# Three weight buffers for the expert layers of a fused transformer, first loads during the token table, held biases, GpSimd on a quarter of the one-hots

## What is computed

```python
for e in range(E):                                  # E = 8, H = 768
    w_e = jnp.sum(top_w * (top_idx == e), axis=-1)
    h = jax.nn.silu(xf @ Wg[e].T) * (xf @ Wu[e].T)
    out = out + h @ Wd[e].T * w_e[:, None]
```

```python
h = jax.nn.gelu(jnp.einsum('bld,df->blf', x, W1e) + b1e, approximate=False)
out = jnp.einsum('blf,fd->bld', h, W2e) + b2e
y = y + ge[..., None] * out
```

## Time and profile before

| | us |
|---|---|
| median of 3 runs | 3250.55 (3246.6 to 3256.33) |
| the profiled execution | 3239.71 |
| its span, first to last instruction | 3238.0 |
| TensorE busy in the span | 2587.4 (80%) |
| VectorE busy | 1416.1 (44%) |
| ScalarE busy | 919.4 (28%) |
| GpSimd busy | 389.2 (12%) |

### The profile page before, as it was taken

How to read it: one execution, slowest core, us unless ns; L and a number is a source line. 1 busy time by engine, 2 the same in 40 slices (tenths; PEclk the granted TensorE clock), 3 DMA queues, 4 the chain that set the end, 5 groups by cost and what they waited for, 6 DMA issues and landing times. The chain is left out here.

```text
span 3238.0 us, 57118 instructions
## 1 busy us (share of the span) xinstructions
PE 2587.4 (80%) x18506; PEld 2223.7 (69%) x18506; DVE 1416.1 (44%) x3924; ACT 919.4 (28%) x2177; POOL 389.2 (12%) x486
## 2 busy tenths in 40 slices
PE   5876999955775688983999368999578989889895
PEld 5774999944664478873888256777357777777775
DVE  2346333345776511114222743555564363453634
ACT  1220222213552133321222113444123242332421
POOL 0000222210000133330000100000011010110100
PEclk8987999977995799995999558999679999999898
DMA  3002333320001355553000000000011203113021
GB/s 87 0 21 63 119 97 110 123 75 14 0 0 39 95 154 152 146 143 69 0 0 0 2 1 14 0 0 1 10 33 44 73 0 87 29 29 87 0 82 35
DMA packets 162395, 164.72 MB, mean 51 GB/s; under 512 B 24040, under 2 KB 147614, under 8 KB 162334
## 3 DMA queue, kind: packets, MB, share of 16 engines
q1 hardware_dynamic: 142334, 130.13, 14.4%
q0 software_dynamic: 11520, 27.54, 2.8%
q10 hardware_dynamic: 8480, 6.29, 0.8%
HBM read 255.23 MB, written 20.45 MB: 85 GB/s over the span
## 5 line engine op out<-in xcount | busy, mean ns | idle before, releaser
L874 PE MATMUL f_pg<-f_vxT,f_w 128*128 128x128 f32 x2112 | 265.2, 281 | 46.1 <-DMA f_b<-in_L_ffn_b 28.6
L874 PEld LDWEIGHTS f_pg<-f_vxT,f_w 128*128 128x128 f32 x2112 | 256.8, 196 | 53.8 <-issue 52.2
L887 PE MATMUL f_po<-f_wd,f_hid 128*128 128x192 f32 x1440 | 255.7, 327 | 13.1 <-DMA f_b<-in_L_ffn_b 7.9
L887 PEld LDWEIGHTS f_po<-f_wd,f_hid 128*128 128x128 f32 x1440 | 231.8, 191 | 16.5 <-ACT f_hid L925 12.3
L2225 PE MATMUL s_bank<-s_disp,s_w 96*128 96x256 f32 x768 | 174.8, 385 | 7.1 <-DVE s_disp L2321 7.1
L925 ACT ACTIVATE f_hid<-f_pg,f_b 128x128 f32<-128x128 f32 x384 | 106.2, 376 | 249.4 <-PE f_pg L880 249.4
L948 DVE TENSOR_TENSOR f_hid<-f_silu,f_pg 128x128 f32<-128x128 f32 x336 | 81.5, 284 | 214.1 <-ACT f_silu L921 199.4
L844 POOL DMA_INDIRECT f_answers<-f_vout,f_to_row x120 | 118.5, 987 | 457.9 <-DVE f_vout L960 248.1
L2236 PE MATMUL s_bank<-s_hid,s_w 128*96 128x256 f32 x768 | 171.0, 379 | 0.0
L2225 PEld LDWEIGHTS s_bank<-s_disp,s_w 96*128 96x128 f32 x768 | 147.9, 193 | 30.4 <-DVE s_disp L2321 8.8
L921 ACT ACTIVATE f_silu<-f_pg 128x128 f32<-128x128 f32 x336 | 78.1, 277 | 301.9 <-PE f_pg L880 281.5
(11 more groups left out here) (372 smaller groups left out, 4916.2 us busy)
## 6 DMA issues: line engine op xcount, KB each, us to landing
f_wd<-in_L_ffn_W SPq DMA_DIRECT2D x64, 576.0 KB
s_w<-in_w SPq DMA_DIRECT2D x128, 288.0 KB, 3.4
f_wd<-in_L_ffn_WdT SPq DMA_DIRECT2D x56, 576.0 KB
f_w<-in_L_ffn_W SPq DMA_DIRECT2D x64, 384.0 KB
f_w<-in_L_ffn_WgT SPq DMA_DIRECT2D x56, 384.0 KB
f_w<-in_L_ffn_WuT SPq DMA_DIRECT2D x56, 384.0 KB
f_wr<-in_L_ffn_W SPq DMA_DIRECT2D x128, 96.0 KB
f_wr<-in_L_ffn_WgT SPq DMA_DIRECT2D x112, 96.0 KB
```

Source lines behind the costliest of these rows:

```text
L874: pe.matmul(pg[j][:, a * ROWS:(a + 1) * ROWS], lift[a][r][:, j * 128:j * 128 + 128], xT[r][:, 0, :], start=(a == 0), stop=False, skip_grou ...
L887: last = pe.matmul(po[:, c * D:c * D + D], hid[r][:, j, c * 128:c * 128 + 128], wd[r][:, j, :], start=(at == 0), stop=(at == FC - 1))
```

## The change

- `fresh` compares with tile n - 3, and each buffer (weights, rows, transposed rows, hidden values, outputs) exists three times.
- A class `Weights` holds the weight buffers over both blocks. In `tokens_of_places` SyncE now runs `begin`, which asks for the weights of tiles 0 to 2, and in f1 all biases of all experts. In `experts` SyncE goes tile by tile: two register reads, wait until tile n - 3 was lifted, lift loads, wait until it was lowered, down load.
- The two halves of the lift weights come with one DMA for 128 partitions instead of two for 64; its DRAM side is read as (half, row, column).
- The biases of f1 aren't loaded per tile. ScalarE and VectorE read the tile's expert into a register and address the held biases with it.
- GpSimd makes at_hi for every odd pair, VectorE for the even ones; VectorE still makes all at_lo. TensorE waits for both.

The core of the diff:

```diff
-            nc.vector.tensor_tensor(passed[:, 2:NT], tile_expert[:, 2:NT], tile_expert[:, 0:NT - 2], ALU.not_equal)
-            link(nc.vector.memset(passed[:, 0:2], 1.0))
+            nc.vector.tensor_tensor(passed[:, 3:NT], tile_expert[:, 3:NT], tile_expert[:, 0:NT - 3], ALU.not_equal)
+            link(nc.vector.memset(passed[:, 0:3], 1.0))
...
+        @block.sync
+        def _(sp):
+            begin(sp)
...
+            pool.wait_ge(ready, 1)
+            for n in range(1, PAIRS_OF, 2):
+                t = n // 2
+                if n >= RINGS:
+                    pool.wait_ge(used, n - RINGS + 1)
+                nc.gpsimd.tensor_scalar(at_hi[n % RINGS][:], iota[0:H2, 0:A], hi[:, 1, t:t + 1], token[:, 1, t:t + 1],
+                                        ALU.is_equal, ALU.mult).then_inc(picked_by_pool, 1)
...
+                if n % 2:
+                    pe.wait_ge(picked_by_pool, n // 2 + 1)
...
-                nc.vector.tensor_scalar(at_hi[n % RINGS][:], iota[0:H2, 0:A], hi[:, r, t:t + 1], token[:, r, t:t + 1],
-                                        ALU.is_equal, ALU.mult).then_inc(picked, 1)
+                last = nc.vector.tensor_scalar(at_lo[n % RINGS][:], iota[0:H2, :], lo[:, r, t:t + 1], None, ALU.is_equal)
+                if r == 0:
+                    last = nc.vector.tensor_scalar(at_hi[n % RINGS][:], iota[0:H2, 0:A], hi[:, r, t:t + 1], token[:, r, t:t + 1],
+                                                   ALU.is_equal, ALU.mult)
+                last.then_inc(picked, 1)
...
-            def bring_lift(n, r, e, new):
-                sp.wait_ge(lifted, (n + 1) * PER)
-                for a, src in enumerate((w_in1, w_in2) if gated else (w_in1,)):
-                    sp.dma_start(lift[a][r][:], src[ds(e, 1), 0:128].rearrange("o p n -> p (o n)"), cond=new).then_inc(loaded[r], 16)
-                    for s in range(2):
-                        sp.dma_start(rest[a][r][64 * s:64 * s + 64],
-                                     src[ds(e, 1), 128:D, s * HALF * 128:(s + 1) * HALF * 128].rearrange("o p n -> p (o n)"),
-                                     cond=new).then_inc(loaded[r], 16)
-                if not gated:
-                    sp.wait_ge(hidden, (n + 1) * FC)
-                    sp.dma_start(bias[r][:], b1[ds(e, 1)].rearrange("o p c -> p (o c)"), cond=new).then_inc(loaded[r], 16)
-            def bring_down(n, r, e, new):
-                sp.wait_ge(lowered, n + 1)
-                sp.dma_start(wd[r][:], w_down[ds(e, 1)].rearrange("o (c p) n -> p (o c) n", p=128), cond=new).then_inc(down_loaded[r], 16)
-                if not gated:
-                    sp.wait_ge(outed, n + 1)
-                    sp.dma_start(down_bias[r][:], b2[ds(e, 1)].broadcast_to([128, D]), cond=new).then_inc(down_loaded[r], 16)
-            def of_tile(n):
-                return (sp.value_load(expert_of[0:1, ds(n, 1)], min_val=0, max_val=E - 1),
-                        sp.value_load(fresh[0:1, ds(n, 1)], min_val=0, max_val=1))
-            bring_lift(0, 0, *of_tile(0))
-            with sp.Fori(0, NT // 2 - 1) as i:
-                e = [of_tile(i * 2 + r) for r in range(3)]
-                bring_lift(i * 2 + 1, 1, *e[1])
-                bring_down(i * 2, 0, *e[0])
-                bring_lift(i * 2 + 2, 0, *e[2])
-                bring_down(i * 2 + 1, 1, *e[1])
-            bring_lift(NT - 1, 1, *of_tile(NT - 1))
-            bring_down(NT - 2, 0, *of_tile(NT - 2))
-            bring_down(NT - 1, 1, *of_tile(NT - 1))
+            def bring(n, r):
+                e, new = weights.of_tile(sp, n)
+                sp.wait_ge(lifted, (n - 1) * PER)
+                weights.bring_lift(sp, r, e, new)
+                sp.wait_ge(lowered, n - 1)
+                weights.bring_down(sp, r, e, new)
+            with sp.Fori(0, (NT - 3) // 3) as i:
+                for r in range(3):
+                    bring(i * 3 + (3 + r), r)
+            for n in range(3 + (NT - 3) // 3 * 3, NT):
+                bring(n, n % 3)
...
-                                            in_offset=bass.IndirectOffsetOnAxis(ap=from_row[:, n * RC + c:n * RC + c + 1], axis=0)
-                                            ).then_inc(rowed[n % 2], 16)
+                if n >= 3:
+
+                    pool.wait_ge(turned, n - 2)
+                pool.indirect_dma_start(out=rows[n % 3][:], out_offset=None, in_=normed,
+                                        in_offset=bass.IndirectOffsetOnAxis(ap=from_row[:, n:n + 1], axis=0)
+                                        ).then_inc(rowed[n % 3], 16)
 
...
+                if not gated:
+                    e = act.value_load(weights.expert_of[0:1, ds(n, 1)], min_val=0, max_val=E - 1)
...
+                    if not gated:
+                        e = dve.value_load(weights.expert_of[0:1, ds(n - 1, 1)], min_val=0, max_val=E - 1)
...
+class Weights:
+    def __init__(self, k, name, ctx, expert_of, fresh, E, w_in1, w_in2, w_down, b1, b2):
+        self.expert_of, self.fresh, self.E = expert_of, fresh, E
+        self.ups = (w_in1,) if w_in2 is None else (w_in1, w_in2)
+        self.w_down, self.b1, self.b2 = w_down, b1, b2
+        self.lift = [[k.sb(f"{name}_w{a}_{r}", [128, FF], ctx=ctx) for r in range(3)] for a in range(len(self.ups))]
+        self.rest = [[k.sb(f"{name}_wr{a}_{r}", [128, FF // 2], ctx=ctx) for r in range(3)] for a in range(len(self.ups))]
+        self.wd = [k.sb(f"{name}_wd_{r}", [128, FC, D], ctx=ctx) for r in range(3)]
+        self.bias = self.down_bias = None
+        if b2 is not None:
+            self.bias = k.sb(f"{name}_b1", [128, E, FC], ctx=ctx)
+            self.down_bias = k.sb(f"{name}_b2", [128, E, D], ctx=ctx)
+        self.loaded = [k.sem(f"{name}_loaded{r}") for r in range(3)]
+        self.down_loaded = [k.sem(f"{name}_down_loaded{r}") for r in range(3)]
+        self.biased = k.sem(f"{name}_biased")
+        self.LOADS, self.DOWN_LOADS = 16 * 2 * len(self.ups), 16
+    def of_tile(self, sp, n):
+        return (sp.value_load(self.expert_of[0:1, ds(n, 1)], min_val=0, max_val=self.E - 1),
+                sp.value_load(self.fresh[0:1, ds(n, 1)], min_val=0, max_val=1))
+    def bring_lift(self, sp, r, e, new):
+        for a, src in enumerate(self.ups):
+            sp.dma_start(self.lift[a][r][:], src[ds(e, 1), 0:128].rearrange("o p n -> p (o n)"),
+                         cond=new).then_inc(self.loaded[r], 16)
+            sp.dma_start(self.rest[a][r][:], src[ds(e, 1), 128:D].rearrange("o p (s n) -> (o s) p n", s=2),
+                         cond=new).then_inc(self.loaded[r], 16)
+    def bring_down(self, sp, r, e, new):
+        sp.dma_start(self.wd[r][:], self.w_down[ds(e, 1)].rearrange("o (c p) n -> p (o c) n", p=128),
+                     cond=new).then_inc(self.down_loaded[r], 16)
+    def begin(self, sp):
+        for n in range(3):
+            e, new = self.of_tile(sp, n)
+            self.bring_lift(sp, n, e, new)
+            self.bring_down(sp, n, e, new)
+            if n == 0 and self.b2 is not None:
+                sp.dma_start(self.bias[:], self.b1.rearrange("e p c -> p e c")).then_inc(self.biased, 16)
+                sp.dma_start(self.down_bias[:].rearrange("p e d -> p (e d)"),
+                             self.b2.rearrange("(o e) d -> o (e d)", o=1).broadcast_to([128, self.E * D])
+                             ).then_inc(self.biased, 16)
...
+        with ExitStack() as held:
+            weights = Weights(k, name, held, expert_of, fresh, E, w_in1, w_in2, w_down, b1, b2)
+            tokens_of_places(k, name, place_of, from_row, to_row, slots, weights.begin)
+            experts(k, name, normed, answers, from_row, to_row, weights, E)
```

More of the change, by code:

```diff
@@ L740, in _, with experts @@
                                            op0=ALU.add, op1=ALU.add)
-def experts(k, name, normed, answers, from_row, to_row, expert_of, fresh, E, ROWS, w_in1, w_in2, w_down, b1, b2):
+def experts(k, name, normed, answers, from_row, to_row, weights, E):
     nc = k.nc
-    gated = w_in2 is not None
+    lift, rest, wd, bias, down_bias = weights.lift, weights.rest, weights.wd, weights.bias, weights.down_bias
+    loaded, down_loaded, LOADS, DOWN_LOADS = weights.loaded, weights.down_loaded, weights.LOADS, weights.DOWN_LOADS
+    ROWS = 128
+    gated = bias is None
     NT = tiles_of(E, ROWS)
-    RC = ROWS // 128
     HALF = FC // 2
@@ L754, in experts, with three @@
     ups = 2 if gated else 1
+    LOOPS = (NT - 5) // 3
     with ExitStack() as ctx:
-        def two(x, shape):
-            return [k.sb(f"{name}_{x}{r}", shape, ctx=ctx) for r in range(2)]
-        lift = [two(f"w{a}_", [128, FF]) for a in range(ups)]
-        rest = [two(f"wr{a}_", [128, HALF * 128]) for a in range(ups)]
-        wd = two("wd_", [128, FC, D])
-        bias = None if gated else two("b1_", [128, FC])
-        down_bias = None if gated else two("b2_", [128, D])
-        rows, xT = two("vrows", [128, RC, WIDE]), two("vxT", [128, 2, ROWS])
```

(40 more changed lines are left out.)

130 lines of the change are left out of this document (61 added, 69 removed).

## The result

| | before | after |
|---|---|---|
| median (range) | 3250.55 us (3246.6 to 3256.33) | 3362.06 us (3349.64 to 3373.15) |
| span of the profiled execution | 3238.0 us | 3371.4 us |
| ratio of the times | | 1.034 (95% interval 1.030 to 1.038) |

Where these 133 us lie is read from five starts: the first matmul of each token table, and the first and last start of a lift weight load of each expert loop.

The account below looks back on a forecast made before the run. It took f1 to be bound by SyncE's issuing and f0 by TensorE. Stalls +180, first loads -6 and token table -11 made +163 us on 3250.6, so 3413 us, range 3300 to 3545.

Parts of the forecast that it names:

- What bounded f1: f1's expert loop: SyncE's issuing bounds it, 12.4 us per pair of fresh tiles against 9.06 us of TensorE.
- The merged load on two engines: Half load in both expert loops: runs on two DMA engines, 98.3 KB each, +180 us of stalls; chance 0.82.
- spread over 16: Rival for the half load in both loops: it uses 16 engines, stalls go, -78 us, 3173 us; chance 0.11.
- Its price: Hot engine's work per fresh tile: 13.4 us in f0, 8.1 in f1, at 23.3 B/ns (lift) and 17.9 (down).
- followers: Newly loaded tiles right behind another: 14 in f0, 6.9 us late each (96 us); 31 in f1, 3.6 (112 us).
- firsts: First newly loaded tile of each burst: f0 2.5 us late, seven times, 17 us; f1 about 1 us at five.
- The clock: Expert loops: TensorE's granted clock may fall after a stall, up to 1.3 us each, mostly hidden; 10 us in all.
- Where the stalls show: Expected signs: waits naming the half load, 14 f0 stalls of 6 to 8 us, DMA share not higher, table 21 us.
- First loads and table, -6 and -11: Starts of both layers: early loads remove first-lift waits, -6 us; GpSimd's share shortens the token table, -5.5 us a layer.
- SyncE's queue held up: Rival in the loops: two engines' backlog delays later loads, 2 us more for 45 fresh tiles, 3500 us; chance 0.04.
- Held biases, nothing: Held biases and value reads on ScalarE and VectorE: cost nothing, or 19 us if the read comes between.
- Third buffer on its own: Expert loops: with SyncE's lighter work it would give back nearly all of f1's 59.5 us and f0's 4.7.

Follow-up runs that it names:

- e6: e1 with f1's two biases loaded per tile by SyncE into each of three buffers, no value reads on ScalarE and VectorE: 3188.99 us, ratio 0.981.
- e1: The changed kernel with the two halves of the lift weights again loaded by two DMAs of 64 partitions each: 3162.97 us, ratio 0.973 to the kernel before.
- e7: The changed kernel with only the gate matrix's halves in two DMAs; f0's up matrix and f1's one matrix stay merged: 3284.68 us, ratio 1.010.
- e3: The kernel before with only the two half loads made one merged DMA: 3358.51 us, ratio 1.033.

## Why the prediction was right, and where its sizes were off

Forecast were 3413 us, slower with a chance of 0.86, range 3300 to 3545; measured 3362. The difference to before was forecast at +163 us and is +112 by the medians, +133 by the spans. The lower bound that the terms gave was 3250.6 + 140 - 17 = 3374 us: the median lies 12 us under it (the profiled execution 10 us over the same bound for it, 3363), and in the range because that reached down to 3300, for which no term was given.

*What bounded f1.* SyncE's issuing did: with the same number of buffers as the change but two more DMAs a tile (e6), 29 us of waits on biases come back. Right, but for the order of the bias load that e6 also changed.

*The merged load on two engines.* Right, and the core of the result: 130 packets a load, 44 to 54 GB/s in the slices, 199 us between the changed kernel and e1, and a pace that follows the bytes when one of two loads is spread (e7). Its rival, spread over 16, was priced at 3173 us; e1, which is that case, gave 3163.

*Its price.* This is the term that was mis-sized. I took 23.3 B/ns for the lift rows and 17.9 for the down rows and had 13.4 and 8.1 us a fresh tile; seen are 11.91 and 7.3. With the same bytes, 297 KB / 11.91 = 24.9 and 174 KB / 7.3 = 23.8 B/ns. An estimate of the split: if the rows of the merged load go at e7's 27 B/ns, their 196.6 and 98.3 KB take 7.3 and 3.6 us, and the other 100 and 76 KB go at 22 and 21 B/ns. The 17.9 was a queue's bytes over its busy share while all 16 engines were loaded; the two busy engines did not go that slowly here. By terms, in f0: 14 followers x (11.91 - 6.54) = 75 us (96 forecast), seven firsts at 8.98 on the mean, 7 x 2.44 = 17 (17 forecast), and the tile behind each burst 8.1 us instead of 6.54, 11 us. Together 103, and the loop of e1 is 103 us shorter. In f1 30 tiles stand 7.0 to 9.1 us apart, +87 us (112 forecast, for 31 followers; there are 32), eight others 5.7 to 6.9, +13 (5 forecast); three of these eight, at 6.2 us, are the tile behind a burst, 5 us.

*The clock.* 10 us forecast. The tiles behind the bursts, whose weights were there, show 11 us in f0 and 5 in f1; TensorE's busy time grew by 34 us in f0, but most of that lies in the shade of the next load, as said. Right in kind, somewhat low.

*Where the stalls show.* f0 was to have 14 stalls of 6 to 8 us. The longest wait was 5.3 us. In intervals the 14 tiles lose 5.4 us each; in the interval from 365.02 to 376.83 us only 3.2 of that was idle time and 1.9 went into the lift at the lower clock. Nor did TensorE wait more in f0 than in f1: 61.7 + 6.8 us against 69.5. The table took 19.5 us, not 21. Of the rest of the list this held: TensorE waits for the half load in both loops, the DMA share didn't grow, SyncE waits for TensorE in f1. How long a gather takes to land isn't told by the trace of after; TensorE's waits for gathered rows in f1 were 9.9 us, 7.7 of them at the first tile, where before they were 6.4 and 5.9.

*First loads and table, -6 and -11.* Their measured sum is -8.1 us. The table itself did better than forecast (6.9 and 7.0 us less, not 5.5 each), but in f0 some 8 us went to the block's end, which waits for SyncE. I had named "SyncE's queue held up" as a rival for the loops and gave no thought to it here. In the loops it is seen too (the issue of a down load took up to 4.32 us; with the halves apart at most 0.39). It added nothing that the sum would need: the fresh tiles keep the pace of the two engines' bytes, beside which SyncE's hold-up runs. No run has the one without the other. Rows of the down loads' issues in f0's loop, after and e1 (ns, min/median/max):

```profile
L1029 SPq DMA_DIRECT2D f_wd<-in_L_ffn_WdT x53: 73/82/4321, 324.7 to 768.1; - x53
```

```profile
L1031 SPq DMA_DIRECT2D f_wd<-in_L_ffn_WdT x53: 79/79/390, 315.6 to 655.9; - x53
```

*Held biases, nothing.* They cost nothing where they are asked for early, and they gain: they are some 26 us of e1's gain. *Third buffer on its own*: not run alone. Of e1's 89.5 us over the kernel before, the table accounts for 11, the early loads for 17.7, the held biases for 26, each as what its removal cost; the 35 or so left are the third buffer and the fewer value reads together, and I can't split them.

*The sum.* On the spans: f0's loop +98.4 where my terms gave about +117, f1's +41.4 where they gave about +62, the starts -8.1 for -17, and +1.7 elsewhere (half of the clock's 10 us counted in each loop).

## What to carry to other kernels

Merging two DMAs into one saves an issue of 0.65 us, but look at the outermost count of both sides first: a count of 2 put 192 KB on two engines and cost 199 us here, more than twice what all the other edits together gave (89 us). In the kernel before, with 16 and 32 loads in place of 24 and 44, it cost 106 us (e3). In this case a low mean DMA share beside long waits for DMA was the sign of it, and the count of closing packets with a stretch at a tenth of share told it apart from a spread load. Loads that are issued inside a block whose end others wait for can get on the path when their queue backs up, as in f0's start here (some 8 us).
